# Rotated keys kept for one batch at a time instead of two, in a fused gated cross-attention and ternary FFN kernel

## What is computed

```python
# x: (2, 512, 512)   ctx: (2, 1024, 128)   16 heads
q_hk   = (layernorm(x) @ Wq.T).reshape(b, s, 16, 128)
q_big  = einsum('bshk,hkq->bshq', q_hk, w_kc_q)        # 384 wide
kv     = ctx * cos + rotate_half(ctx) * sin            # rotated context
q_r    = einsum('bshq,hqr->bhsr', q_big, W_qr)         # 64 wide queries
k_r    = einsum('bld,hdr->bhlr', kv, W_kr)             # 64 wide keys
attn   = softmax(einsum('bhsr,bhlr->bhsl', q_r, k_r))  # 512 x 1024 per head
ctx_c  = einsum('bhsl,bld->bhsd', attn, kv)
out    = (ctx_c @ w_kc_kv per head) @ Wo.T
x      = x + tanh(g_xattn) * out
x      = x + tanh(g_ffn) * ffn(layernorm(x))           # quantized activations, ternary weights
```

## Time and profile before

| | before |
|---|---|
| median of three runs | 756.39 us |
| the profiled execution | 756.84 us |
| its span on the core | 755.0 us |
| TensorE matmul busy | 721.8 us (96%) |
| VectorE busy | 590.5 us (78%) |
| ScalarE busy | 481.1 us (64%) |
| GpSimd busy | 238.8 us (32%) |
| DMA, mean over the span | 63 GB/s |

### The profile page before, as it was taken

How to read it: one execution, slowest core, us unless ns; L and a number is a source line. 1 busy time by engine, 2 the same in 40 slices (tenths; PEclk the granted TensorE clock), 3 DMA queues, 4 the chain that set the end, 5 groups by cost and what they waited for, 6 DMA issues and landing times.

```text
span 755.0 us, 12561 instructions
## 1 busy us (share of the span) xinstructions
PE 721.8 (96%) x4058; PEld 515.5 (68%) x4058; DVE 590.5 (78%) x1012; ACT 481.1 (64%) x807; POOL 238.8 (32%) x221
## 2 busy tenths in 40 slices
PE   3899999999999999999999999999999999998997
PEld 3676768676867686768677867777777676644553
DVE  5777867777778677767888888888887899999873
ACT  2566656666566656665666665666576766478876
POOL 4812222121222222222222222222222234676751
PEclk9999999999999999999999999999999999999999
DMA  8301140104010401040114111321120001000001
GB/s 291 119 5 57 42 139 29 57 29 154 28 56 28 153 28 56 28 153 29 56 56 151 60 56 56 108 100 56 48 79 19 27 2 56 1 1 15 29 29 43
DMA packets 21394, 47.69 MB, mean 63 GB/s; under 512 B 3952, under 2 KB 7152, under 8 KB 21232
## 3 DMA queue, kind: packets, MB, share of 16 engines
q1 hardware_dynamic: 20176, 45.49, 17.7%
q10 hardware_dynamic: 1120, 1.77, 0.7%
q0 software_dynamic: 64, 0.00, 0.0%
HBM read 45.16 MB, written 2.10 MB: 63 GB/s over the span
## 4 chain that ended last, share of the span: by engine, by line
PE 77%; DVE 11%; issue 5%; ACT 5%; DMA 1%; POOL 1%; ACTq 0%; DVEq 0%; POOLq 0%
PE ps_b L1257 12%; PE ps_s L1204 11%; PE ps_ctx L1215 8%; PE ps_b L1178 7%; PE ps_ctx L1217 6%; PE ps_ctx L1216 6%; PE ps_s L542 4%; PE ps_b L1127 4%; PE ps_b L1125 4%; PE ps_b L1126 4%; DVE small L1534 2%; PE ps_b L1157 2%; PE ps_b L593 2%; DMA wqr_s<-in_wqr 1%; PE ps_b L1149 1%
## 5 line engine op out<-in xcount | busy, mean ns | idle before, releaser
L1058 POOL TENSOR_SCALAR E<-E,small 128x1024 f32<-128x1024 f32 x128 | 148.3, 1159 | 444.2 <-DVE small L1539 444.2
L1349 ACT ACTIVATE et_hi<-ps_b 128x512 fp32r<-128x512 f32 x256 | 153.2, 602 | 184.5 <-PE ps_b L1257 184.5
L1495 DVE TENSOR_TENSOR et_lo<-ps_b,et_hi 128x512 fp32r<-128x512 f32 x256 | 175.4, 685 | 52.8 <-ACT et_hi L1349 50.5
L1534 DVE TENSOR_REDUCE small<-ps_s 128x1 f32<-128x1024 f32 x128 | 155.6, 1217 | 6.7 <-PE ps_s L1204 4.7
L1257 PEld LDWEIGHTS ps_b<-ident,E 128*128 128x128 f32 x1024 | 124.7, 140 | 52.2 <-issue 15.8
L1257 PE MATMUL ps_b<-ident,E 128*128 128x128 f32 x1024 | 154.0, 273 | 3.5 <-DVE q_lo L1495 2.0
L1383 ACT ACTIVATE E<-ps_s,small 128x1024 f32<-128x1024 f32 x128 | 142.9, 1116 | 13.5 <-DVE small L1534 12.9
L1215 PE MATMUL ps_ctx<-et_hi,kv_hi 128*128 128x512 f32 x256 | 120.8, 472 | 0.4 <-DVE ctx_lo L1495 0.2
L1217 PE MATMUL ps_ctx<-et_lo,kv_hi 128*128 128x512 f32 x256 | 101.2, 395 | 0.0
L1216 PE MATMUL ps_ctx<-et_hi,kv_lo 128*128 128x512 f32 x256 | 100.5, 393 | 0.0
L1215 PEld LDWEIGHTS ps_ctx<-et_hi,kv_hi 128*128 128x128 f32 x256 | 48.3, 189 | 24.8 <-issue 16.6
(11 more groups left out here) (174 smaller groups left out, 1016.2 us busy)
## 6 DMA issues: line engine op xcount, KB each, us to landing
w_stage<-in_wffn SPq DMA_DIRECT2D x48, 512.0 KB, 3.4
wo_s<-in_woT SPq DMA_DIRECT2D x8, 512.0 KB, 6.0
wq_s<-in_wq SPq DMA_DIRECT2D x7, 512.0 KB, 5.8
wkcq_s<-in_wkcqT SPq DMA_DIRECT2D x7, 384.0 KB, 3.9
x_sb<-in_x SPq DMA_DIRECT2D x4, 512.0 KB, 12.1
out<-x_sb SPq DMA_DIRECT2D x8, 256.0 KB, 2.0
wqr_s<-in_wqr SPq DMA_DIRECT2D x7, 192.0 KB, 4.6
wkv_s<-in_wkv SPq DMA_DIRECT2D x8, 128.0 KB, 5.0
```

What stands on the lines that cost most here:

```text
L1058: nc.gpsimd.tensor_scalar(e, e, rowinv[:, k:k + 1], 1.0, ALU.mult, ALU.mult).then_inc(scaled, 1)
L1349: return nc.scalar.activation(out, in_, ACT.Copy)
L1495: return nc.vector.tensor_tensor(out, full, hi.bitcast(F32), ALU.subtract)
L1534: nc.vector.tensor_reduce(negmax[:, k:k + 1], ps_s[:, t % 2, :], AX_X, ALU.max, negate=True).then_inc(max_done, 1)
```

## The change

The key buffers hold one batch. Batch 1's keys of pair p are made in unit 0 of pair p itself (steps 3 and 4), once the last scores of batch 0 have been issued, and batch 0's keys of pair p + 1 are made in unit 2 (steps 3 and 4). Queries of batch 0 move from unit 1, step 2, to unit 2, step 0; queries of batch 1 stay at unit 3, step 1. The prologue loses its two key tasks of batch 1. To make room, the outputs of the pair before move from steps 4 and 5 of unit 0 to steps 5 and 6, task ("b", 0) moves from step 6 to step 7 of unit 0, and the outputs of unit 1 move from steps 4 and 5 of unit 2 to steps 5 and 6. ScalarE's copy into the keys gets a wait for the scores that still read them. The last pair keeps its key tasks of batch 1.

```diff
 SIDE = [
-    {0: ("m",), 2: ("a",), 4: ("out", 3, 0), 5: ("out", 3, 1), 6: ("b", 0)},
-    {0: ("b", 1), 2: ("q", 0), 4: ("out", 0, 0), 5: ("out", 0, 1)},
-    {0: ("k", 0, 0), 1: ("k", 0, 1), 4: ("out", 1, 0), 5: ("out", 1, 1)},
-    {0: ("k", 1, 0), 1: ("q", 1), 2: ("k", 1, 1), 4: ("out", 2, 0), 5: ("out", 2, 1)},
+    {0: ("m",), 2: ("a",), 3: ("k", 1, 0), 4: ("k", 1, 1), 5: ("out", 3, 0), 6: ("out", 3, 1), 7: ("b", 0)},
+    {0: ("b", 1), 4: ("out", 0, 0), 5: ("out", 0, 1)},
+    {0: ("q", 0), 3: ("k", 0, 0), 4: ("k", 0, 1), 5: ("out", 1, 0), 6: ("out", 1, 1)},
+    {1: ("q", 1), 4: ("out", 2, 0), 5: ("out", 2, 1)},
 ]
...
-        behind = task[0] in ("m", "a", "k", "q")
+        behind = task[0] in ("m", "a", "q") or task[:2] == ("k", 0)
...
-PROLOGUE_TASKS = [("m",), ("a",), ("k", 0, 0), ("k", 0, 1), ("q", 0, 0), ("q", 0, 1), ("q", 1), ("k", 1, 0), ("k", 1, 1)]
+PROLOGUE_TASKS = [("m",), ("a",), ("k", 0, 0), ("k", 0, 1), ("q", 0, 0), ("q", 0, 1), ("q", 1)]
...
-        k_hi = sa("k_hi", [P, BATCH, LCTX], F32R)
-        k_lo = sa("k_lo", [P, BATCH, LCTX], F32R)
+        k_hi = sa("k_hi", [P, LCTX], F32R)
+        k_lo = sa("k_lo", [P, LCTX], F32R)
...
-                pe.wait_ge(wk_ready, 1 if at is not None else p + 2)
-                if at is not None:
+                pe.wait_ge(wk_ready, 1 if at is not None else p + 2 - b)
+                if at is not None or variant == "first" and b == 1:
                     pe.wait_ge(kvt_ready, 2 * b + j + 1)
...
-                        if (w + ahead, half) == (2, 0) and not is0(p):
-                            pe.wait_ge(side_freed, side_index(p, "mid", max(BATCH1, key=ORDER["mid"].get)) + (1 - SIDE_PER_PAIR))
+                        if (w + ahead, half) == (2, 0):
+                            pe.wait_ge(side_freed, side_index(p, variant, ("k", 1, 1)) + 1)
...
-                last = copy_act(k_hi[:, b, cols], bank_in)
+                if at is None:
+                    act.wait_ge(scores_done, 16 * p + (8 if b else 16))
+                last = copy_act(k_hi[:, cols], bank_in)
...
-            task(7)
-            pe.wait_ge(side_freed, 7)
-            task(8)
             pe_pair(pe, 0, "first")
```

More of the change, by code:

```diff
@@ L99, in side_tasks @@
     return {c - early: task for c, task in SIDE[w].items() if wanted(task)}
-PROLOGUE_TASKS = [("m",), ("a",), ("k", 0, 0), ("k", 0, 1), ("q", 0, 0), ("q", 0, 1), ("q", 1), ("k", 1, 0), ("k", 1, 1)]
+PROLOGUE_TASKS = [("m",), ("a",), ("k", 0, 0), ("k", 0, 1), ("q", 0, 0), ("q", 0, 1), ("q", 1)]
 CTX_BANK = 3
-PRO_BANK = (0, 1, CTX_BANK, 0, 2, 0, CTX_BANK, 0, CTX_BANK)
+PRO_BANK = (0, 1, CTX_BANK, 0, 2, 0, CTX_BANK)
 PRO_INDEX = {t: i for i, t in enumerate(PROLOGUE_TASKS)}
@@ L1203, in score_matmuls @@
                         head = slice(h * R, (h + 1) * R)
-                        last = nc.tensor.matmul(ps_s[:, h, cols], q[head, b, rows], k[head, b, cols],
+                        last = nc.tensor.matmul(ps_s[:, h, cols], q[head, b, rows], k[head, cols],
                                                 start=(i == 0), stop=(i == 2))
@@ L1224, in wait_bank @@
                 if variant == "first" and bank_of(variant, user) == 0:
-                    pe.wait_ge(side_freed, PRO_INDEX["k", 1, 0] + 1)
+                    pe.wait_ge(xnt_copied, TT)
+                elif variant == "first":
+                    pe.wait_ge(kvt_ready, bank_of(variant, user) + 2)
             elif before[0] == "turn":
@@ L1511, in side_low @@
                 cols = slice(j * NF, (j + 1) * NF)
-                last = lo_part(k_lo[:, b, cols], bank_in, k_hi[:, b, cols])
+                last = lo_part(k_lo[:, cols], bank_in, k_hi[:, cols])
             elif kind == "q":
```

## The result

The changed kernel is slower: 766.5 us, the median of four runs (766.36 to 768.77), against 756.43 us (756.02 to 757.04) for the kernel before on the same chip. The ratio is 1.0136, with a 95% interval of 1.0121 to 1.0151. The profiled execution took 766.48 us, with a span of 764.7 us (before 756.84 and 755.0).

What follows compares the result with a forecast made beforehand. The prediction took TensorE's own work to set a pair's time. Its terms summed to +10.65 us, less 1.65 for small waits, so +9: 765.8 us for the profiled execution, 765.4 as a median, range 760 to 769.

Steps and rivals of the forecast that it cites:

- The place and the mechanism: Unit 1: turn T3 waits for b_lo of head 1, ending 3.07 us after T1, in all eight pairs; 80 in 100.
- The loss in unit 1: Start of unit 1: late b_lo, second exponential and ctx_lo cost 1.75, 1.6 or 1.5 us a pair, +13.3 us.
- what the Trainium skill says: Unit 1: wk_lo waits out GpSimd's scaling, both reading SBUF; without it 0.1 us falls away, 0.7 us in seven pairs.
- Unit 3: T3 no longer needs the bank of the queries just written; seven waits of 0.55 us go, -3.9 us.
- The start: Prologue: first pair begins 1.65 us earlier, with 1.40 us more key work behind that point, -0.25 us.
- +2.4: Start of unit 2: queries at step 0 delay ScalarE's second exponential, 0.35 us in each of seven pairs.
- −1.7: Unit 2: the three k_lo waits behind key tasks at steps 0 and 1 go away, a gain of 1.7 us.
- +0.8: Key tasks at steps 3 and 4: T5 sometimes gets its bank 0.2 to 0.4 us late, +0.8 us taken.
- waits too small to be listed: Beside the key tasks of units 2 and 3: waits under 0.16 us go away, estimated at 1.65 us.
- taken up at all by slack: Rival on unit 1: slack absorbs the late b_lo and the change is faster, 753.7 us; 5 in 100.
- Half of it: Rival on unit 1: part of the lag is caught up, +13.3 becomes +6.5, 758.6 us; 10 in 100.
- Keys were not late: Rival: scores wait for batch 1's keys in all fifteen places, 1 us each, 780 us; 5 in 100.

Runs made afterwards that it cites:

- The first: The changed kernel with b of head 0 moved to step 0 and b of head 1 to step 1 of unit 1: 750.46 us.
- second: The changed kernel with b of head 1 moved from step 0 to step 2 of unit 1: 764.33 us.
- fourth experiments: The kernel before with only b of head 0 moved from step 6 to step 7 of unit 0: 767.09 us.
- the last experiment: The kernel before with b of head 0 moved to step 0 and b of head 1 to step 1 of unit 1: 755.51 us.
- the first four experiments: Changed kernel: both b at unit 1's steps 0, 1, 750.46 us; second b later, 764.33; queries back in unit 1, 769.76. Kernel before: first b later, 767.09.
- the last four: Changed kernel: key weights' split later, 767.15 us; two-batch buffers, no wait, 766.8; both b in unit 1, queries at unit 2's step 2, 748.28. Kernel before: both b moved, 755.51.
- the experiment with the key weights: The changed kernel with the next key weights' split at step 3 of unit 1 instead of step 1: 767.15 us.

## Why the prediction was right, step by step

**The place and the mechanism** were right. b_lo of head 1 ends 3.11 us after T1 (predicted 3.07), T3 starts 3.16 after it (3.13), the scores 0.86 after T3 (0.86). The view of waits has b_lo eight times, 9.6 us. The first, second and fourth experiments show it from three sides: take the first b away from step 7 (with the second a step on) and the cost goes, leave the bank alone and it stays, bring that b alone into the kernel before and the cost comes.

**The loss in unit 1** measured 14.7 us against +13.3: 1.91 to 1.97 a pair instead of 1.75, 1.79 instead of 1.6, 1.56 instead of 1.5. The missing 0.2 us a pair is one link: the product behind the scores is 0.29 us late, not 0.1 (144.10 − 142.22 = 1.88, where 1.59 is enough). GpSimd's scaling starts 3.98 us after T1, where I had 3.80, and wk_lo ends with it. The prediction also weighed what the Trainium skill says (SBUF — State Buffer, section Who interferes with whom), that such an instruction of VectorE is blocked for the whole of GpSimd's. The traces agree for the most part. Beside the scaling wk_lo ends 0.13 to 0.14 us after it and takes 0.78 to 1.20 us, by how late it starts; moved away from the scaling it takes 0.28 us, and the whole 0.3 us a pair falls away. But the one that starts first in the trace is not always the one that is spared: in five pairs of the first and the last experiment wk_lo started 0.07 us after the scaling, took 0.29 us, and the scaling took 1.26 to 1.28 us in place of 1.12; in three others of the same two it started as close behind and was held.

**Unit 3**, −3.9: measured −3.5, 0.50 us a pair. The rows themselves gave 0.68 − 0.23 + 0.06 = 0.51; I had counted 0.55. **The start**, −0.25: VectorE's first maximum begins 1.14 us after kv_lo in place of 2.84, so 1.70 us earlier (predicted 1.65), and by unit 1 of pair 0 TensorE is 1.60 us ahead: the 1.09 us told of below, and 0.51 us in place of the 0.25.

**Unit 2 and the key tasks** were three terms, +2.4, −1.7 and +0.8. The wait behind the exponential is there: scores 2.44 us after T1 (predicted 2.43), 0.20 us of it visible. The key tasks hardly wait: once, 0.2 us, in pair 7, whose unit 0 grew by 0.38 us beyond its keys. Together units 0 and 2 came to −0.4 us, where the three terms say +1.5. Most of the difference is what I had set apart as waits too small to be listed, −1.65, an estimate that had only its order of size behind it. The traces of unit 2 bear it out. Less the keys' 1.40 and the queries' 3.44 us, the scores of step 3 start 3.52 us after T0 before and 3.55 after in pair 1, and 3.90 and 3.55 in pair 5: the waits beside the keys, most of them unlisted, were as large as the new wait for the exponential, and in pair 5 0.35 us larger.

**The sum.** Measured: −0.5 at the start, +14.7 in unit 1, −0.7 in unit 2, −3.5 in unit 3, +0.3 in unit 0, +0.1 in the last unit of pair 7 and +0.3 behind the last turn, in the FFN: 10.7 us. The span grew by 9.6 us, because 1.1 us came back in the prologue for another reason. Predicted were 9 us: unit 1 was 1.4 too low, unit 3's gain 0.4 too high, the last 0.4 not foreseen, and the start and units 0 and 2 came out 0.5 better. So part of the agreement of the two times (765.8 predicted, 766.48 measured for the profiled execution) is luck: the prologue's 1.1 us hid most of an error of 1.7. The FFN's 0.3 us go with a fall of the granted clock, told of below. And one step of the prediction's arithmetic doesn't come out: its bounds add up to +2.4 (10.4 − 8) and +16.7 us (16.8 + 2.8 + 3 − 5.9), not to +3 and +13, so the range of 760 to 769 was narrower than its own terms, at the upper end above all. The measured loss lies well inside either.

**The rivals.** The lag was not taken up at all by slack: b_lo came within 0.04 us of the predicted time. Half of it was not taken up either: unit 1 lost more than predicted. Keys were not late: no score at step 7 waits.

## What to carry to other kernels

On engines that each run their own queue in order, ask what a side task puts ahead of a reduction in a neighbour's queue, and what that item itself waits for. In this kernel the task cost most where its low part stood ahead of the maximum, and least where it stretched TensorE beside the maxima: the two b tasks one step later gave 16 us back, and the first of them one step later than before had cost 10. (Whether VectorE's maximum taken ahead of b_lo at step 0 would do as well was not tried.) When a task has to make room for others, work out the neighbour's queue over the next three steps at its new place first. And ask of each place that a move empties what chain the task had been covering: an empty unit start made TensorE wait 1.1 us, more than the 0.35 that a task at its first step delays the exponential; at the third step the same task covered the chain and delayed nothing.

## What the runs showed of the hardware

The 1.1 us in the prologue come from eight plus eight transposes just after the first matmuls. The timeline of TensorE, before first, then the changed kernel:

```profile
14.75 1.91 PE L1302 MATMUL ps_s<-ident,E 128*128 128x128 f32 x8
16.45 1.50 PE L1294 MATMUL ps_s<-ident,wq 128*128 128x128 f32 x8
```

```profile
14.79 1.21 PE L1306 MATMUL ps_s<-ident,E 128*128 128x128 f32 x8
15.84 1.05 PE L1298 MATMUL ps_s<-ident,wq 128*128 128x128 f32 x8
```

The first eight took 1.92, 1.59, 1.84 and 1.83 us in the first four experiments and 1.91, 1.11, 1.91 and 1.92 in the last four. Six of these eight have the changed kernel's prologue, and 1.11 to 1.92 us are among them, all with the granted clock listed as 1.00, so the time differs from one execution to the next and not by the kernel. The second eight took 1.04 us in three of the experiments and 1.86 in one. So near the start TensorE's pace can differ by almost a factor of two while the clock is listed as full; the cause stays open. A difference of 1 us between two single profiles of this kernel is therefore not yet an effect.

The falls of the granted clock were the other surprise: the same wait of 1.2 us stands in eight places of the changed kernel, and in its profiled execution the clock stayed at 1.00 behind each of them (its one fall is at 694 to 698 us, in the FFN), while behind two of the eight in the experiment with the key weights it halved for about 3 us. So a wait in a dense stretch may cost 1.5 us more than itself, and not in every execution. The wait alone doesn't decide it: five of the traces have eight such waits for b_lo, and behind 38 of the 40 the clock stayed at 1.00. What does is not shown. The fall in the FFN is in five of the ten traces. From pair 7's last turn to the end of the span these five take 103.99 to 104.18 us, the other five 103.86 to 103.91.
